# A new order table for the loop of the first attention: batch b's second half against batch b+1's first half, on four engines

## The reference

```python
q, k, v = x @ Wq, x @ Wk, x @ Wv              # heads of 8
w = l2norm(silu(conv3(x @ wA @ wB)));  beta = 2 * sigmoid(x @ beta_w);  g = log_sigmoid(x @ g_w + g_b)
q, k = rmsnorm(q), rmsnorm(k)
L = tril(w w^T * beta, -1) + I;  A = solve_triangular(L, tril(w k^T, -1))
S = q k^T - tril(q w^T) (beta A)
logits = S * scale + G_i - G_j                 # G = cumsum(g), causal
o = softmax(logits) @ v;  return o @ Wo
...
x = x + ga * attention(layernorm(x) * (1 + ca) + sa)
```

## Time and profile before

| | us |
|---|---|
| median of 3 runs (lowest, highest) | 2446.88 (2429.71, 2449.88) |
| the profiled execution | 2452.07 |
| its span, first to last instruction | 2450.3 |
| mean granted TensorE clock | 0.881 |
| the loop's seven passes together | 1288.6 |

### The profile page before, as it was taken

One profiled execution on the slowest core, in us unless ns is written; L12 is line 12 of the kernel. 1 busy time (PEld: TensorE's weight loads), 2 busy tenths in 40 slices (PEclk: granted clock), 3 DMA queues, 4 the chain that ended last, 5 costly groups with the idle time before them and its releaser, 6 DMA issues. The chain is left out here.

```text
span 2450.3 us, 44308 instructions
## 1 busy us (share of the span) xinstructions
PE 2086.4 (85%) x16522; PEld 1385.6 (57%) x16530; DVE 1590.8 (65%) x3446; ACT 857.6 (35%) x1690; POOL 972.0 (40%) x999
## 2 busy tenths in 40 slices
PE   3888988988988988988988989997899982778885
PEld 2573563563563563563563577766899971334443
DVE  5958668658659568568568655633433334889996
ACT  2031231231231331331331222230465543477782
POOL 2513313413314314313313424844555558875221
PEclk7897997998898998998997988878999985889997
DMA  3103003003003003003003000115222221110000
GB/s 103 35 2 87 1 3 86 1 3 86 1 3 86 1 3 86 1 3 86 1 3 86 1 21 29 42 34 197 64 73 71 72 77 42 38 32 27 5 9 13
DMA packets 136617, 98.83 MB, mean 40 GB/s; under 512 B 14753, under 2 KB 127586, under 8 KB 136290
## 3 DMA queue, kind: packets, MB, share of 16 engines
q1 hardware_dynamic: 128226, 79.21, 11.0%
q0 software_dynamic: 8192, 16.79, 2.2%
HBM read 36.25 MB, written 55.57 MB: 37 GB/s over the span
## 5 line engine op out<-in xcount | busy, mean ns | idle before, releaser
L606 ACT ACTIVATE a_prep<-ps 128x1536 f32<-128x1536 f32 (+1 forms) x112 | 155.7, 1390 | 435.3 <-PE ps L1219 243.1
L833 DVE TENSOR_REDUCE a_mpart<-ps 128x4 f32<-128x512 f32 x320 | 199.4, 683 | 52.3 <-PE ps L1160 36.5
L419 POOL TENSOR_TENSOR a_X<-a_X,a_txy 128x480 f32<-128x480 f32 (+14 forms) x240 | 181.8, 767 | 107.6 <-DVE a_txy L787 105.2
L413 POOL TENSOR_TENSOR a_K<-a_K,a_yU 128x480 f32<-128x480 f32 (+14 forms) x120 | 83.6, 696 | 339.4 <-DVE a_yU L782 339.4
L1759 ACT ACTIVATE b_hid<-ps,b_stage 128x128 f32<-128x128 f32 x576 | 164.2, 368 | 139.7 <-PE ps L1863 139.7
L1743 POOL COPY b_stage<-b_w 128x1028 f32 x144 | 150.1, 1044 | 128.0 <-PE ps L1872 128.0
L1038 PE MATMUL ps<-a_txy,cst 128*128 128x480 f32 (+14 forms) x480 | 174.5, 466 | 11.2 <-DVE a_txy L769 10.8
L2003 POOL DMA_INDIRECT c_got<-rows_y,packed x128 | 150.7, 1177 | 38.3 <-issue 35.5
L1863 PE MATMUL ps<-b_hTp,b_stage 128*128 128x128 f32 x1152 | 154.0, 278 | 0.0
L1872 PE MATMUL ps<-b_stage,b_hid 128*128 128x128 f32 x1152 | 152.5, 276 | 0.3 <-ACT b_hid L1759 0.3
L1436 POOL DMA_INDIRECT rows_h<-a_tS,r_slot x112 | 110.2, 984 | 103.9 <-issue 52.1
(11 more groups left out here) (469 smaller groups left out, 4576.6 us busy)
## 6 DMA issues: line engine op xcount, KB each, us to landing
rows_h<-a_blank SPq DMA_DIRECT2D x66, 512.0 KB, 6.1
b_hrow<-rows_h SPq DMA_DIRECT2D x144, 64.0 KB, 1.8
rows_y<-b_orow SPq DMA_DIRECT2D x144, 64.0 KB, 1.5
b_w<-in_wexp SPq DMA_DIRECT2D x16, 514.0 KB, 10.9
c_got<-rows_y,packed POOLq DMA_INDIRECT x128, 2.5
out<-xs SPq DMA_DIRECT2D x8, 256.0 KB, 2.3
cst<-in_const SPq DMA_DIRECT2D x1, 1865.5 KB, 14.6
rows_h<-a_tS,r_slot POOLq DMA_INDIRECT x112, 2.2
```

The costliest lines, as they stand in the source:

```text
L419: nc.gpsimd.tensor_tensor(x, x, yX[:, a, 0:n].rearrange("p (c s) -> p c s", c=NC), ALU.subtract).then_inc(e_uX.sem, 1)
L606: nc.scalar.activation(Pt[:, at:at + width, :], ps[:, 4:4 + width, :], ACT.Exp).then_inc(e_exp.sem, width)
L833: nc.vector.tensor_reduce(mpart[:, i, j, 4 * g:4 * g + 4], ps[:, 4 + n % 4, :].rearrange("p (r j) -> p r j", r=4), AX.X, ALU.max).then_inc ...
```

## The change

The four strings of `ORDER` (PE, VectorE, ACT, POOL) are replaced. What each engine issues stays the same; only how the steps of `back` and `front` alternate is new. SP's instructions are the same in the same order.

```diff
 ORDER = {
-    'pe': ('bbbbbbbbfbbbfbbfbfbbbbfffbbbbbbbbbbfbbbbbbbfffbbbbbbbbbbbffbbbbbfbbbbbbffbbbbffbbbbbbbbbbbfbbfbbffbb'
+    'pe': ('bbbbbbbbbfbbbbfbfbfbbbfffbbbbbbbbbbfbbbbbfffbbbbbbbbffbbbfbbbfbbbbfffbbbbbbffbbbbbffbbbbbbbbbbfbbbbb'
...
-    've': ('fbfbfbbbbffbfffffbbfbffffbbffffffffbbbbfffbbbbfffbbbbfffbbbbffbbbbffbbbbffbbfbbffbbbbffbbbbffbbbbfbf'
+    've': ('fbbfbfbbbbfffffffbbfbffffbfbfffffffffffbbbbffffbbbbffffbbbbffffbbbbffbbbbffbbbbffbbbbffbbbbffbbbbffb'
...
-    'act': ('bbffbfbbffbffbbfffffbbbfbfffbbfbbfbbbbbbbbbbbbbbbbbbbbbffbbbb'),
-    'po': ('bbbbbbbffffffffffffbfffbfbbbfbbbfbffffffffffffffffffffffffffffff'),
+    'act': ('bbffbbfbbfffbfbfffffbbbffbfffbfbbfbbbbbbbbbbbbbbbbbbbbbfbfbbbb'),
+    'po': ('bbbbbbbfffffffffffffffbfffbfbbbfbbfbbfffffffffffffffffffffffffff'),
 }
```

More of the change, by code:

```diff
@@ L133 @@
 ORDER = {
-    'pe': ('bbbbbbbbfbbbfbbfbfbbbbfffbbbbbbbbbbfbbbbbbbfffbbbbbbbbbbbffbbbbbfbbbbbbffbbbbffbbbbbbbbbbbfbbfbbffbb'
-           'bbbbbbbbffbffbbfbbbbbbbbbfbbbfbbbfbbbbbbbbfffbbbbbbbffbbbbffbbfbbbbbbbbffbbbbbbffbbbbfffbfbbfbbfbbff'
-           'bbfbfffbbbbfbfbffbbbbbffffbbbffbbbbffbbffffbbbbbffbfbbbbbbbfbbbbbbbfbbbbbbbbbfbbbbfbb'),
-    've': ('fbfbfbbbbffbfffffbbfbffffbbffffffffbbbbfffbbbbfffbbbbfffbbbbffbbbbffbbbbffbbfbbffbbbbffbbbbffbbbbfbf'
-           'bfbbbfbfbfffffbbfbbbbbbbbfbbbbbbbbbfbbbfbfffbffffffffbfbfffffffbffffffffffffffffffffffffffffffffffff'
-           'fffbfffffffffffffffffffffffffbbbbbfbbbbfffbb'),
-    'act': ('bbffbfbbffbffbbfffffbbbfbfffbbfbbfbbbbbbbbbbbbbbbbbbbbbffbbbb'),
-    'po': ('bbbbbbbffffffffffffbfffbfbbbfbbbfbffffffffffffffffffffffffffffff'),
+    'pe': ('bbbbbbbbbfbbbbfbfbfbbbfffbbbbbbbbbbfbbbbbfffbbbbbbbbffbbbfbbbfbbbbfffbbbbbbffbbbbbffbbbbbbbbbbfbbbbb'
+           'fbfbbbbfbbbbfbffbbffbbbbbbbbbfbbbfbbbfbfbfbbfbbbfbfbbbfffbbfbfbbbfbffbfffbbbbbbbffbffbbbbbbbbbfffbbb'
+           'bbbbfffbbbbfbfbbfbbbbbbbfffbbbbbbbfffbbbbbbbfffbbbbbbbfbbbbbbbfbbbbbbbbbfbbbbbbbfbfbb'),
+    've': ('fbbfbfbbbbfffffffbbfbffffbfbfffffffffffbbbbffffbbbbffffbbbbffffbbbbffbbbbffbbbbffbbbbffbbbbffbbbbffb'
+           'bbbfbfbfbbbfbfbffffffbbfbbbbbbbbfbbbbbbffbfbfbbbbffbfffbffffffffffffffffffbfffbfffffffffffbfffffffff'
+           'ffffffffffffbffffffffffffffbbbbbbfffbbbfffbb'),
+    'act': ('bbffbbfbbfffbfbfffffbbbffbfffbfbbbbbbbbbbbbbbbbbbbbbbbfbfbbbb'),
+    'po': ('bbbbbbbfffffffffffffffbfffbfbbbfbbfbbfffffffffffffffffffffffffff'),
 }
```

## The result

| | before | after |
|---|---|---|
| median of 3 runs (lowest, highest), us | 2446.88 (2429.71, 2449.88) | 2416.86 (2415.09, 2421.09) |
| span of the profiled execution, us | 2450.3 | 2419.3 |
| the seven passes together, us | 1288.60 | 1252.58 |
| ahead of them / behind them, us | 144.2 / 1017.5 | 146.0 / 1020.7 |

The ratio is 0.9886, 95% interval 0.9846 to 0.9926, so 1.1% less; the medians lie 30 us apart. The time lies in the range on record (2399 to 2470) and 10 us under the forecast of 2427. The loop gave 36.0 us, 5.15 per pass; in the two profiled executions 5 us came back outside it, where no instruction was moved.

What follows compares the result with a forecast made beforehand. TensorE bounds the kernel, wholly so behind the first score. Scores start 1.4 us later with 4.2 less behind them; less 0.3, plus 0.3, gives 2.8 per pass, 19.6 over seven: 2427 us, range 2399 to 2470.

Steps and rivals of the forecast that it cites:

- the slow clock behind the start of the scores: First score to end of pass: 74.2 us taken as PE work, falling to 70.0 by the 4.2 moved ahead.
- the idle time that was to be filled: Ahead of the first score: each idle PE us filled saves one; second pass idle 11 to 12 instead of 14.6.
- Rival (a): Less idle time ahead of the scores also shortens slow-clock stretches: 2 to 4 us more per pass, 2399 to 2413; chance 0.16.
- Scores at 109.5 to 110 in the second pass: First score (L1210) expected 109.5 to 110 us into the second pass, where it was 108.5.
- Worth little: Before the maxima: L1001 and L1005 ahead of L1130 start the first matmul between 1.4 us and not at all sooner.
- End of the maxima stage 1.0 later: Maxima stage: VectorE gets net 1.9 us more work, so the stage ends 1.0 us later.
- First spread 0.3 sooner behind it: Turning the maxima: the wait behind POOL's Qsm copies stays, with U 320 replacing U 352, for 0.3 us less.
- Spreads 0.7 longer: The 16 spreads: three more VectorE operations cost about 1.2 us, partly in existing idle room; 0.7 counted.
- The price on both sides: VectorE's two-input operations and GpSimd's reads exclude each other: tX 288 twice between POOL's adds, up to 1.4 us later.
- Scores and tail, idle 0.3 more: Behind the first score: smaller fronts leave short waits and the tail's builds shift; 0.3 us more PE idle counted.
- Rival (b): Maxima and spreads lengthen by all they take in; scores 4 us later, 2447 (2438 to 2460); with (d), chance 0.26.
- Rival (c): Maxima stage: alternating PE and VectorE waits fall into the slow clock; 3.8 us lost per pass, 2474; chance 0.16.

Runs made afterwards that it cites:

- e5: e2 with five unread 128x512 matmuls in PE's two gaps, ahead of the first score and of the second group; 2471.5 us, 1.0085 of before.
- e9: e4 with five unread 128x256 matmuls in PE's gap ahead of L1001, on another chip; 2493.2 us, 0.9816 of before's 2536.0 there.
- e1: New order from the start of a pass to the first reduction (L833), the order before from there on; 2453.1 us, 1.0041 of before.
- e4: The changed kernel with the four masked copies Qsm made by ScalarE instead of POOL; 2406.9 us, 0.9840 of before.
- e6: e4 with VectorE's tU of width 352 ahead of the last four reductions instead of behind them; 2410.6 us, 0.9840 of before.
- e3: Order before up to the first score, new order behind it, six moved front steps in a row at the scores' beginning; 2445.1 us, 1.0000 of before.
- e2: New order up to the first score (L1210), the order before behind it without front steps already done; 2501.0 us, 1.0203 of before.
- e10: The changed kernel once more, unaltered, on another chip; 2494.1 us, 0.9821 of before's 2536.0 there.
- e11: e4 once more, unaltered, on another chip; 2497.3 us, 0.9842 of before's 2536.0 there.

## Why the prediction was right, and where its sizes were off

Per pass the forecast was 1.4 later at the first score, 4.2 less work behind it: 2.8. Measured: 1.9 later; at full clock a stretch 3.47 shorter; 3.5 less slow clock in it: 5.1. So the direction was right, and the moved work was (4.6 of busy time for 4.2), but the forecast's own account gave 1.6 us a pass, 11 us in all, and the clock the larger part. That the time came 10 us from 2427 is partly luck, and the range was wide enough to hold no change at all.

Two steps failed. **The one that counts was set to nothing, the slow clock behind the start of the scores** ("Behind the start of the scores PE thus has 4.2 less to do: 70.0 instead of 74.2."). The 74.2 held 4.4 us of slow clock on average of the passes, and the new order has 0.9. The evidence was there: the stretch stood at a granted clock of 0.95 with PE full, and 74.2 was taken as work. **The other is the idle time that was to be filled** ("An idle us filled before 438.3 is a us less at the end"). Ahead of the first score PE idles for 1.1 us a pass less than before, and behind it for 1.2 more: over the pass none was filled, 19.5 and 19.6. Windows of the second pass up to the turned maxima, before and after:

```profile
329.80:424.80 95.00, 80.21 (x549) 44.53 (x551) 73.47 (x122) 29.10 (x58) 30.80 (x26) 0.84 0.20 57
```

```profile
324.00:418.80 94.80, 81.18 (x557) 46.56 (x558) 76.46 (x128) 27.81 (x57) 32.22 (x29) 0.85 0.21 57
```

- *Rival (a), the clock gives more*, had the size, 2 to 4 us a pass, and the wrong place. It looked for it in less idle time ahead of 438.3. There the second pass idles for 13.6 us by these windows (14.8 before, which the prediction has as 14.6), where it said 11 to 12, and the slow clock ahead of the first score cost about the same (14.7 us a pass, then 14.3). The Trainium skill, page TensorE: Matmul & The Clock Gate, section "What's actually happening", has activity release the throttle; e5 agrees with it at its two gaps, and e9, on few passes, at its own. The stretch at 1029 shows half speed behind 10 us of full activity.
- *Scores at 109.5 to 110 in the second pass*: 108.4, for 108.5 before. That pass was longer than most up to its scores; the mean went from 106.2 to 108.0.
- *First reduction at 42*: 42.5. *L1001's wait near 2*: 2.24. *Worth little*: e1, a loss of 0.4% (0.1 to 0.7).
- *End of the maxima stage 1.0 later*: 2.2. e1, which adds nothing to the stage, makes it 1.1 longer at a lower clock (0.79 for 0.85), so part of it may be the clock (0.82 after); how much isn't shown.
- *First spread 0.3 sooner behind it*: 0.7. POOL's wait was 3.00 there and is 1.45 now; a second one, 2.88 ahead of L1173, is that of VectorE's reductions (e4, e6).
- *Spreads 0.7 longer*: 0.4. The price on both sides is there in part: tX 320 took 0.78 each beside POOL's two-input updates (L413, L419), but tX 352 took 0.52 while POOL made the Qsm copies (L434), which take one input tile.
- *Scores and tail, idle 0.3 more*: 1.2 more, 2.6 of 69.2.
- *Rival (b), paid in full*, has e3's time (1.0000 of before), but in another place: the scores start 7.5 us later and the stretch behind them is 7.3 shorter. Moved as a block, the steps give nothing. *Rival (c)*, slower through the clock, did not come about here; it is e2, by a mechanism nobody had named: gaps at the start of the scores that the front no longer covers.
- *Range and chances*: with 36 us in the loop and 5 lost outside it, the time fell into the lower part, under 2422, which had 0.39.

What starts the slow stretches in the full part of the scores stays open. That they go with the alternation, and not with how much work is left there, is borne out by e3 and e5 (0.98 and 0.92 of the clock); why the new one has fewer is not known, and no third alternation was tried.

## What to carry to other kernels

Divide a full stretch's time into work and slow clock before moving anything: passes of the same instructions, laid side by side, differ in equal steps, and the shortest is the work. When work is moved out of a stretch to fill gaps elsewhere, see what covered the gaps at the stretch's own start; in e2 such waits of 2.3 and 1.6 us, and the slow clock that goes with them, were part of 12 us lost a pass: filling them with useless work gave 4 back. And a wait that names a tile may be the queue in front of the operation that makes it: look at what its engine did in that time, not at the tile.

## What the runs showed that was not expected

- Up to L1271's start the last stretch takes one of a few lengths: 66.37, 67.96 and 69.53 us with the new order, 69.84 to 76.11 in steps of 1.5 to 1.6 with the old. Which, changes from pass to pass in one execution.
- Five wide matmuls added to a pass made e2 30 us faster.
- On the other chip e10's seven passes took 1250.8 us, as on the first (1252.6), but what lies behind them 1111.0 instead of 1020.7. In the profiles the whole difference sits between the loop's end and the first expert (L1743): 359 to 370 us in e9, e10 and e11, 273 to 279 before, after and in e4. From there to the end all six take 741. The ratios to before agree on both chips.
